# A graph attention layer on one core: how the rows of 3 edge tiles of 16 are fetched, and where the turned destination one-hots are made

## What is computed

```python
Qh = (x @ Wq.T + bq).reshape(n, H, D)            # H = 4, D = 16
Kh = (x @ Wk.T + bk).reshape(n, H, D)
Vh = (x @ Wv.T + bv).reshape(n, H, D)
Ee = (edge_attr @ We.T + be).reshape(-1, H, D)
score = (Kh[src] * Qh[dst] * (1.0 / np.sqrt(D)) * Ee).sum(-1)
score = jnp.exp(jnp.clip(score, -5.0, 5.0))
msg = Vh[src] * score[..., None]
wV = jax.ops.segment_sum(msg, dst, num_segments=n)
x = _layernorm(x + wV.reshape(n, H * D))
```

## Time and profile before

| what | value |
|---|---|
| time, median of 3 runs | 2893.62 us (2882.82 to 2894.67) |
| profiled execution: span | 2801.3 us |
| profiled execution: its own time | not given; the median of the runs is 92.3 us above the span |
| TensorE busy | 1925.7 us, 69% |
| VectorE busy | 1174.3 us, 42% |
| ScalarE busy | 851.7 us, 30% |
| GpSimd busy | 1400.8 us, 50% |

### The profile page before, as it was taken

One profiled execution on the slowest core, in us unless ns is written; L12 is line 12 of the kernel. 1 busy time (PEld: TensorE's weight loads), 2 busy tenths in 40 slices (PEclk: granted clock), 3 DMA queues, 4 the chain that ended last, 5 costly groups with the idle time before them and its releaser, 6 DMA issues. The chain is left out here.

```text
span 2801.3 us, 49920 instructions
## 1 busy us (share of the span) xinstructions
PE 1925.7 (69%) x16647; PEld 1663.0 (59%) x16647; DVE 1174.3 (42%) x2092; ACT 851.7 (30%) x2863; POOL 1400.8 (50%) x1495
## 2 busy tenths in 40 slices
PE   4666677777767667776767676667676667766775
PEld 4555666666656556665656665656565656655665
DVE  4433444444434444444444444434344444434444
ACT  6222222332223223223322222223232223222233
POOL 5444554455554445555445555445545545555443
PEclk7777777777778777787877877778778777778776
DMA  6222222222222222222222222222222222222221
GB/s 194 63 56 57 59 58 58 57 61 57 58 54 59 56 58 60 58 59 59 59 57 58 59 57 58 57 56 60 57 58 58 59 57 60 59 58 59 56 61 45
DMA packets 113024, 171.42 MB, mean 61 GB/s; under 512 B 59952, under 2 KB 60592, under 8 KB 112880
## 3 DMA queue, kind: packets, MB, share of 16 engines
q0 software_dynamic: 46848, 96.04, 13.5%
q1 hardware_dynamic: 66160, 75.18, 9.8%
HBM read 163.85 MB, written 7.23 MB: 61 GB/s over the span
## 5 line engine op out<-in xcount | busy, mean ns | idle before, releaser
L275 POOL DMA_INDIRECT kv<-kv_table,idx x1464 | 1384.4, 946 | 1351.1 <-DVE idx L303 944.9
L675 PE MATMUL xg_bank<-x_parts,src_onehot 128*128 128x192 bf16 x7252 | 904.6, 286 | 102.7 <-issue 99.1
L675 PEld LDWEIGHTS xg_bank<-x_parts,src_onehot 128*128 128x128 bf16 x7252 | 739.8, 115 | 187.4 <-issue 129.2
L803 DVE TENSOR_TENSOR src_onehot<-src_ps,columns 128x1664 bf16<-128x1664 bf16 (+1 forms) x592 | 573.0, 968 | 537.0 <-remote 359.3
L646 PE MATMUL qe_ps<-q_win,onehot_t 128*128 128x128 bf16 x2418 | 250.2, 267 | 407.2 <-issue 389.9
L646 PEld LDWEIGHTS qe_ps<-q_win,onehot_t 128*128 128x128 bf16 x2418 | 194.3, 120 | 441.2 <-issue 439.5
L735 ACT COPY onehot_t<-oht_bank 128x512 bf16<-128x512 bf16 x202 | 118.0, 584 | 1099.3 <-remote 1052.4
L743 ACT ACTIVATE distance<-iota_w,dst_neg 128x64 f32<-128x64 f32 x1612 | 405.9, 337 | 15.4 <-PEq L306 15.4
L656 PE MATMUL sum_ps<-onehot,msg 128*64 128x64 f32 x3224 | 357.7, 290 | 49.3 <-issue 42.4
L656 PEld LDWEIGHTS sum_ps<-onehot,msg 128*64 128x64 f32 x3224 | 319.8, 200 | 111.1 <-issue 93.8
L844 DVE TENSOR_TENSOR msg<-kv,sum_ps 128x512 f32<-128x512 f32 x202 | 138.0, 683 | 563.2 <-ACT sum_ps L772 497.0
(11 more groups left out here) (117 smaller groups left out, 760.9 us busy)
## 6 DMA issues: line engine op xcount, KB each, us to landing
attr_sb<-attr SPq DMA_DIRECT2D x201, 256.0 KB
kv<-kv_table,idx POOLq DMA_INDIRECT x1464
q_win<-q_table SPq DMA_DIRECT2D x404, 24.0 KB
kv_table<-kv_stage SPq DMA_DIRECT2D x7, 448.0 KB, 3.6
q_table<-q_stage SPq DMA_DIRECT2D x7, 336.0 KB
xT_sb<-xT SPq DMA_DIRECT2D x7, 224.0 KB, 4.8
kv_stage<-x_own_rows SPq DMA_DIRECT2D x1, 1568.0 KB
out<-y_sb SPq DMA_DIRECT2D x5, 256.0 KB, 2.0
```

Source lines behind the costliest of these rows:

```text
L275: pool.indirect_dma_start(out=kv[:, slot, t, :], out_offset=None, in_=kv_table, in_offset=bass.IndirectOffsetOnAxis(ap=idx[:, slot, t:t + ...
L675: mm = pe.matmul(xg_ps[k % 2], src_onehot[:, c, :], x_parts[:, c, :, :], start=(c == 0), stop=(c == NT - 1))
L803: dve.tensor_tensor(src_onehot[:, PARTS[part], :], src_ps.unsqueeze(1).to_broadcast([P, n, P]), columns[:, PARTS[part], :], ALU.is_equal). ...
```

## The change

- **Tiles.** POOL leaves the last two tiles of the even slots and the last one of the odd slots to TensorE: 6, 7, 6 and 7 gathers in four groups. Groups 0 and 1 and the last ones are fetched by POOL alone.
- **One-hots over blocks.** A node number is split in a block of 896 nodes (7 blocks) and a place in it, of 128 x 7. SP loads the places of a tile's sources as a row spread over all partitions (`r_row`), and VectorE makes seven one-hots from it in one instruction. TensorE multiplies each by the features of all 7 blocks, 448 columns, for each of three bf16 parts: 21 matmuls (`gather_x`). VectorE then keeps the columns of each edge's own block (`select_x`: a product with a comparison, and a sum).
- **Turning and projecting** take float32 rows, for one or two tiles at a time. `project` of group g+1 now stands behind `sum_messages` of group g.
- **Destination one-hots, turned.** SP loads the destinations as rows spread over 64 partitions, twice; ScalarE makes `onehot_t` from them with a square and a Relu, for group g+2. TensorE's transposes, `oht_bank` and `src_ps` are gone, and `qe_ps` has two banks.
- **Indices.** SP loads the indices of a group into `idx` when the slot's gathers have landed; POOL waits for them and for the messages of group g.

```diff
-        def pe_tile(g, slot):
-            return slot != 2 and not (isinstance(g, int) and (g < 3 or g >= ITERS * SLOTS))
+        def pe_tiles(g, slot):
+            return 0 if isinstance(g, int) and not PE_FROM <= g < PE_END else 2 - slot % 2
...
                     def gather_next(g, slot):
-                        pool.wait_ge(slot_ready, g - SLOTS + 1)
+                        pool.wait_ge(idx_loaded[slot], 16 * i)
+                        pool.wait_ge(msg_made, g - SLOTS + 1)
                         pool.sem_inc(gathers_begun, 1)
                         gather(pool, g, slot)
...
-                    def gather_part(q, k, part):
-                        pe.wait_ge(src_onehot_made, q * 4 + (part + 1))
-                        for c in range(PARTS[part].start, PARTS[part].stop):
-                            mm = pe.matmul(xg_ps[k % 2], src_onehot[:, c, :], x_parts[:, c, :, :],
-                                           start=(c == 0), stop=(c == NT - 1))
-                        mm.then_inc(x_gathered, 1)
+                    def gather_x(q, parity):
+                        pe.wait_ge(src_onehot_made, q + 1)
+                        xg = bank(xg_banks[parity], F * V)
+                        for u in range(U):
+                            for s in range(3):
+                                mm = pe.matmul(xg, src_onehot[:, parity, u, :], x_parts[s][:, u, :],
+                                               start=(u == 0 and s == 0), stop=(u == U - 1 and s == 2))
+                        mm.then_inc(x_gathered, 1)
...
+                        if not last:
+                            multiply_edges(g + 1, i + (j + 1) // SLOTS, (j + 1) % SLOTS)
+                            fetch_q(g + 1, i + (j + 1) // SLOTS, (j + 1) % SLOTS)
+                        ahead = pe_tiles(g + 2, (j + 2) % SLOTS)
+                        for k in range(ahead)[0:1]:
+                            gather_x(first_q(i, j + 2), (PE_BEFORE[(j + 2) % SLOTS] - PE_SKIPPED) % 2)
+                        turned = pe_tiles(g + 1, (j + 1) % SLOTS)
+                        if turned:
+                            turn_x(g + 1, i, j + 1)
+                        sum_messages(g, j)
+                        if turned:
+                            project(g + 1, j + 1)
+                        for k in range(ahead)[1:2]:
+                            gather_x(first_q(i, j + 2) + 1, (PE_BEFORE[(j + 2) % SLOTS] - PE_SKIPPED + 1) % 2)
...
-                    def keep_onehot(g):
-                        n = pairs_of(g)
-                        act.wait_ge(onehot_turned, g + 1)
-                        act.copy(onehot_t[:, 0:n, :], oht_ps[:, 0:n, :]).then_inc(onehot_t_made, 1)
+                    def make_onehot_t(g, i, slot):
+                        n = pairs_of(g) * P
+                        act.wait_ge(dst_row_loaded[slot], 32 * (i + 1))
+                        act.activation(dst_square[:, 0:n], dst_row[:, slot, 0:n], ACT.Square,
+                                       bias=minus_row[:, ds(g, 1)]).then_inc(dst_squared, 1)
+                        act.wait_ge(dst_squared, g + 1)
+                        act.activation(onehot_t[:, slot % 2, 0:n], dst_square[:, 0:n], ACT.Relu, bias=1.0, scale=-1.0)\
+                           .then_inc(onehot_t_made, 1)
...
+                    def select_x(g, i, j, k):
+                        dve.wait_ge(x_gathered, q + 1)
+                        dve.scalar_tensor_tensor(out=x_sel[:, :, :].rearrange("p f v -> p (f v)"), in0=iota_v[:, :],
+                                                 scalar=src_block[:, ds(q, 1)], in1=bank(xg_banks[parity], F * V),
+                                                 op0=ALU.is_equal, op1=ALU.mult).then_inc(x_selected, 1)
+                        dve.wait_ge(x_selected, q + 1)
+                        dve.tensor_reduce(xg_sb[:, j % 2, k, :], x_sel[:, :, :], AX_X, ALU.add).then_inc(x_summed, 1)
```

More of the change, by code:

```diff
@@ L579, in load @@
                           .then_inc(attr_loaded[slot], 16)
+                        for half in range(2):
+                            rows = slice(half * W, (half + 1) * W)
+                            sp.dma_start(dst_row[rows, slot, 0:n],
+                                         dst_rows[ds(g, 1), half, 0:n].to_broadcast([W, n]))\
+                              .then_inc(dst_row_loaded[slot], 16)
                         base = sp.value_load(base_i[0:1, ds(g, 1)], min_val=0, max_val=BASE_MAX)
@@ new lines, in turn_x @@
+                    def turn_x(g, i, j):
+                        k = pe_tiles(g, j % SLOTS)
+                        pe.wait_ge(x_summed, first_q(i, j) + k)
+                        if not (isinstance(g, int) and g == PE_FROM):
+                            pe.wait_ge(pe_kv_made, g - PE_FROM)
+                        for n in range(k):
+                            mm = pe.matmul(turn_bank[0:F, n, :], xg_sb[:, j % 2, n, :], ident[:, :], start=True, stop=True)
+                        mm.then_inc(x_turned, 1)
@@ new lines, in square_distances @@
+                    def square_distances(g, first, end):
+                        n = 2 * pairs_of(g)
+                        if first == 0 and not (isinstance(g, int) and g == 0):
+                            act.wait_ge(onehot_made, g)
+                        for t in range(first, min(end, n)):
+                            made = act.activation(distance[:, t, :], iota_w[:, :], ACT.Square,
+                                                  bias=dst_neg[:, ds(g, 1), t:t + 1].rearrange("p o t -> p (o t)"))
+                            if t == n - 1:
+                                made.then_inc(distance_made, 1)
@@ new lines, in step @@
+                        if turned:
+                            act.wait_ge(kv_projected, g - (PE_FROM - 2))
+                            if not (isinstance(g, int) and g + 1 < SLOTS):
+                                act.wait_ge(msg_made, g - SLOTS + 2)
+                            act.copy(kv[:, (j + 1) % SLOTS, T - turned:T, :], turn_bank[:, 2:2 + turned, :])\
+                               .then_inc(pe_kv_made, 1)
+                        if ahead:
+                            square_distances(g + 2, T // 2, T)
+                            make_onehot(g + 2, slot2)
```

485 lines of the change are left out of this document (239 added, 246 removed).

## The result

Beside the kernel before, the changed kernel took 2805.07 us (median of 4; 2767.7 to 2824.17) for 2889.91 (2882.82 to 2894.67): a ratio of 0.9667, interval 0.9605 to 0.973. It is faster, by 3.3% where 14% was forecast. All later sessions gave other times for the same two programs: before 1892.5 to 1893.8 us in each of five sessions on four chips, and, in the one of them where both ran, the changed kernel 2036 us, slower by 7.6%. The chip of the first session is not on record. Experiments explain the later result. Of the first, two traces show why a group takes no less time; where the 3.3% come from they do not show.

A forecast was written before the change was run, and what follows sets the result against it. TensorE completion signals, late while gathers are in flight, were taken as the bound. Groups fall from 13.56 to 11.5 us (23.0 per pair), saving 2.06 x 202 = 416 us: 2893.6 - 416 = 2478, say 2480; range 2200 to 2900.

The forecast's parts named there:

- these 92.3: Microseconds by which the median run of the kernel before exceeded its profiled span; kept unchanged in the forecast time.
- (a): POOL's gathers: 29 per four groups become 26, so bursts are 0.94 us shorter in the mean.
- (b): Start of a burst: POOL waits for the message product itself; first gather 0.8 us after it, of 1.79 before.
- (c): Turned one-hots made on ScalarE from loaded rows: the bounding signal goes; costs nothing, 0.6 us per group if uncovered.
- (d): New TensorE signals on the path: projected rows taken as nearly prompt, second tile's gather_x as released with the burst.
- the prompt row at 2.1 us: In before's timeline, acc added at 1472.25, promptly after the sum's matmuls, 2.1 us into its burst; used as evidence.
- The first rival: Projected rows' signals stuck in each 7-gather group until its burst is out: 15.7 us there, 2922 us total; chance 0.12.
- (e): VectorE's one-hot, selection and sum: 2.2 us per tile, 3.3 us per group against 2.9 before; under 7 us per group.
- (f): TensorE: 4.3 us a tile at the high clock, tiles doubled to 1.5 per group; 21.2 us per pair of groups.
- The second rival: Signals not late because of gathers, only TensorE's work counts: 10.6 us per group, saves 598, 2296 us; chance 0.13.
- (g): Loads of rows and indices per group on SP's queue: hidden.
- (h): Before the loop: 13 small VectorE instructions hidden behind the early gathers; nothing.

The follow-up runs named there:

- before_again: The kernel before, unchanged, run again in a later session: 1893.1 us.
- after_again: The changed kernel, unchanged, run again in a later session: 2036.1 us, 1.076 of the kernel before beside it.
- one_tile: Changed kernel with one TensorE tile and 7 POOL gathers in every group: 1981.2 us, 1.046 of the kernel before beside it.
- one_tile_ts: Changed kernel with one TensorE tile per group and the one-hot made by 7 comparisons with a per-partition scalar: 1848.3 us, 0.976 of the kernel before.
- plain: Changed kernel with each indirect gather replaced by a plain DMA of 128 consecutive rows: 2031.8 us, 1.073 of the kernel before beside it.

## Why the prediction was right or wrong

**The baseline (the last step of the sum).** "I let these 92.3 stand" was wrong: the time around the span is 1.8 to 1.9 us wherever a run has both. Of the forecast's 416 us the runs saved 85, and between the two traces nothing was saved. That the runs are 3.3% faster is therefore no success of the mechanism, and what it comes from is not shown.

**(a), (b) Right.** A gather starts each 1.25 us, and a burst 0.78 us after the message product has ended (1434.07 for 1433.29), where 0.8 was taken.

**(c) Right.** ScalarE's wait for the turned one-hots is gone and nothing took time in its place: its exponential (L749) waits for the clip, 26.7 us in the whole run.

**(d) The step that failed.** "If TensorE is free" put the record of the projection 1.6 to 2.8 us after the message product, or 0.8 to 2.0 us into a burst, and "I take it as nearly prompt" followed from that. TensorE was not free. A gather_x stands ahead of turn_x and the sum in its order: in the step shown it ran from 1431.38 for 5.5 us, and the projection started only at 1438.32, 5.0 us after the end of the message product (1433.29) and 4 us into the burst. In the median of the steps with 7 gathers the projection was recorded as done 4.3 us after the message product; in those with 6 it was 2.3 and 2.7, as forecast.

Where in a burst a signal is recorded made the difference in the first session. Of those that another engine of the changed kernel waited for, the ones recorded in the first 2 us of a burst came 0.04 to 0.14 us later in the median, and those recorded 3 to 5 us into it 4.3 to 5.3 us later; in before's trace the sum's signal, early in a burst, took 0.14 us in the median and that of the transposes 4.3 to 4.7. So the prompt row at 2.1 us did not cover the projection.

The first rival's step came true: from the starts of all message products, the medians of a step with 7 gathers are 15.9 and 15.7 us, for its 15.7; those of a step with 6 are 11.6 and 11.7, for the 11.7 of my own sum. Their mean, 13.7 a group, is the rival's (13.5 to 13.6 over the whole stretch). The forecast had 11.5. In the steps with 7 gathers the copy starts 2.6 us after the start of the last gather in the median, for a forecast release of 2.7. That the release comes with the burst is what the trace of the first session shows; no experiment tested it, since the lateness never came back. (The sum's "seen 3 us after msg, 7.9" is moreover 3 + 4.7 = 7.7; that changes nothing here.)

**The premise.** "Completion signals get through slowly while gathers are in flight" is not a property of gathers. before_again has a gather each 1.25 us without a gap, and ScalarE's copy of the turned one-hots follows TensorE's record at once: 1004.47 to 1004.50 in its trace. What differs between the first session and the others is not found. Both kernels were slow in it, so it is not the change. The DMA queues spent the same time on the gathers (13.5% of 2801 us and 19.8% of 1891 us, both 374 to 378 us of 16 engines; for the changed kernel 320 us in the first session and 399 in after_again), so slower transfers are not it. Late signals and TensorE's unexplained stops ("issue", 162.4 and 155.3 us in two lines; above 0.35 us none in after_again and 4 in before_again) came together. Whether one caused the other, or a third thing both, stays open. The rule of the Trainium skill that I had set aside ("SBUF — State Buffer", section "Who interferes with whom": a DMA never contends with a compute engine) agrees with the later traces as far as TensorE goes, as in the 0.04 us above; of the first session it explains nothing.

**(e) Right in its parts.** One-hot 1.08 us for 1.0; selection and sum 0.68 + 0.62 = 1.3 for 1.2. What it left out is that the one-hot keeps a gather waiting, 0.8 us in a group of one_tile. The Trainium skill has this in "SBUF — State Buffer", section "SBUF: two separate sides": a VectorE operation with two inputs from SBUF and a GpSimd operation that reads SBUF exclude each other for a whole instruction. The traces agree: a gather that started within the two-input comparison took 1.75 us in the median of one_tile, and one within a comparison of one tile and a scalar 0.94 in one_tile_ts. So does plain, whose transfers have no indices to read and were not held.

**(f) Right in size, and it decided elsewhere.** 4.3 us a tile at the high clock was 4.1; the pair's 21.2 us was 19.3 in after_again (2 x 9.67). The clock rose to 0.90 and 0.98 in the mean, as forecast. But no case of mine let the kernel before fall too. With prompt signals it is bound by POOL at 9.06 us and not by its signals at 13.56, so that the lighter POOL and heavier TensorE of the change cost 0.6 to 0.7 us a group, 143 us in all. The second rival had the condition of the later sessions right and its sign wrong for that reason. POOL's busy share, which was to rise to 53% with a shorter span, fell to 47%.

**(g), (h) Right.** No wait for a load of any size in the loop.

## What to carry to other kernels

A period explained by late signals should be worked out a second time with prompt ones, for both kernels: here that sum, from rows at hand (7.25 x 1.25 against 21.2 / 2 and VectorE's 7), gives the other sign. How early a result is recorded depends on what stands ahead of it in its engine's order: "if TensorE is free" left a gather_x of 4 to 5.5 us out. An execution's time is compared with its own span before anything is laid on top. A change that moves work from POOL to TensorE is worth the distance between the two bounds: here, with prompt signals, 3 tiles in 4 groups left TensorE some 2 us of room, 6 overran it, and 4 with a one-hot that leaves POOL alone were the best of the versions that keep all three parts.

## What the runs showed of the hardware

- The same program (before) took 1893 us on four chips in later sessions for 2890 in the first, a third less, with POOL's, VectorE's and ScalarE's instructions at the same durations (a gather 0.95 us in both). TensorE's awaited signals came 0.04 to 0.14 us after the record in the median, in the midst of bursts too (after_again). In the first session those of the changed kernel were as prompt in the first 2 us of a burst, and 4.3 to 5.3 us late in the median at 3 to 5 us.
- VectorE's comparison with two inputs from SBUF (1.08 us) held an indirect gather that started inside it by up to 0.9 us (one_tile). Comparisons with one tile from SBUF and a scalar (7 of 0.3 us each, one_tile_ts) held 335 such gathers by 0.14 us at most, and the two-input one did not hold plain transfers (plain).
- The mean granted clock of TensorE was 0.98 in after_again, where TensorE was busy for 97% of the span, 0.91 in before_again at 81%, and 0.77 in the first trace of before at 69%.
